# Moving one PSUM copy behind four exponentials in ScalarE's order, in both attention loops

## What is computed

```python
x = x + tanh(g_xattn[0]) * _L0_xattn_ref(_layernorm(x), ctx, ctx, mask, ...)
x = x + tanh(g_ffn[0]) * _L0_ffn_ref(_layernorm(x), ...)       # 64 experts, top 6
x = x + tanh(g_xattn[1]) * _L1_xattn_ref(_layernorm(x), ctx, ctx, bias, ...)
x = x + tanh(g_ffn[1]) * _L1_ffn_ref(_layernorm(x), ...)       # 8 experts, each takes its best tokens
# in both attentions:
scores = einsum('bhqd,bhkd->bhqk', qh, kh) / sqrt(8)           # masked, or with a bias
attn = softmax(scores, axis=-1)
out = einsum('bhqk,bhkd->bhqd', attn, vh)
```

## Time and profile before

| | |
|---|---|
| three timed runs | 939.1 us median (938.69 to 942.69) |
| the profiled execution | 940.7 us |
| its span, first to last instruction | 938.9 us |
| busy, whole span | PE 77%, DVE 72%, POOL 65%, ACT 52% |
| stretch 81 to 231 us (rolled part of loop 0, 150.00 us): busy | PE 138.50, DVE 136.74, ACT 123.28, POOL 104.03 us |
| stretch 481 to 647 us (rolled part of loop 1, 166.00 us): busy | PE 152.36, DVE 139.83, POOL 136.61, ACT 132.58 us |
| granted TensorE clock | 0.99 in the first of these stretches, 1.00 in the second |

### The profile page before, as it was taken

How to read it: one execution, slowest core, us unless ns; L and a number is a source line. 1 busy time by engine, 2 the same in 40 slices (tenths; PEclk the granted TensorE clock), 3 DMA queues, 4 the chain that set the end, 5 groups by cost and what they waited for, 6 DMA issues and landing times. The chain is left out here.

```text
span 938.9 us, 23770 instructions
## 1 busy us (share of the span) xinstructions
PE 719.0 (77%) x6259; PEld 494.9 (53%) x6259; DVE 673.6 (72%) x2225; ACT 492.1 (52%) x1719; POOL 611.7 (65%) x1109
## 2 busy tenths in 40 slices
PE   3888999999847998358999999999810379879770
PEld 2555556566533666335666666666510157557560
DVE  3787999999966664147888888888769756775334
ACT  2886888878831112037777787777700032432320
POOL 4888666666633676367888888888310376777772
PEclk9999999999967999579999999999955589999895
DMA  6111222222222333133334444333100225665568
GB/s 178 61 66 52 83 83 87 75 75 75 93 66 71 104 106 102 34 114 126 119 118 140 139 142 141 126 125 123 71 12 0 72 52 161 185 167 165 164 182 235
DMA packets 98731, 100.61 MB, mean 107 GB/s; under 512 B 24511, under 2 KB 76077, under 8 KB 98659
## 3 DMA queue, kind: packets, MB, share of 16 engines
q1 hardware_dynamic: 88306, 88.25, 30.2%
q0 software_dynamic: 6656, 9.66, 3.7%
q10 hardware_dynamic: 3696, 1.84, 0.7%
HBM read 60.84 MB, written 44.17 MB: 112 GB/s over the span
## 5 line engine op out<-in xcount | busy, mean ns | idle before, releaser
L563 ACT ACTIVATE P<-bank,mx 128x120 f32<-128x120 f32 x1024 | 277.5, 433 | 4.0 <-DVE mx L865 3.9
L466 PE MATMUL bank<-ident,P 128*120 128x128 f32 x1024 | 167.4, 286 | 41.6 <-ACT P L563 39.3
L466 PEld LDWEIGHTS bank<-ident,P 128*120 128x120 f32 x1024 | 106.1, 138 | 131.2 <-issue 75.2
L865 DVE TENSOR_REDUCE mx<-bank 128x4 f32<-128x480 f32 x256 | 150.5, 650 | 20.8 <-PE bank L455 17.3
L1748 POOL DMA_INDIRECT xg<-token_rows,tokens x64 | 66.7, 1042 | 70.1 <-DVE tokens L1802 51.2
L446 PE MATMUL bank<-bp,identr 128*128 128x480 f32 x256 | 87.3, 426 | 0.0
L1758 POOL DMA_INDIRECT expert_sums<-y,sum_rows x64 | 70.6, 1103 | 23.5 <-issue 18.6
L665 POOL TENSOR_TENSOR Km<-Kf,kmask 128x480 f32<-128x480 f32 x64 | 63.3, 989 | 29.8 <-ACT Kf L547 29.1
L480 PE MATMUL bank<-PT,Vb 120*32 120x128 f32 x2048 | 82.3, 279 | 0.0
L630 POOL TENSOR_TENSOR rstd<-rs,minus_half 128x1 f32<-128x1 f32 x128 | 72.6, 567 | 10.7
L575 ACT ACTIVATE PT<-bank,kept 120x512 f32<-120x512 f32 x64 | 45.2, 706 | 57.8 <-issue 43.0
(11 more groups left out here) (244 smaller groups left out, 1707.7 us busy)
## 6 DMA issues: line engine op xcount, KB each, us to landing
expert_sums<-zeros SPq DMA_DIRECT2D x32, 512.0 KB, 3.4
choice_rows<-zeros SPq DMA_DIRECT2D x32, 384.0 KB, 2.4
yrows<-choice_rows SPq DMA_DIRECT2D x32, 384.0 KB, 3.1
XT<-expert_sums SPq DMA_DIRECT2D x16, 512.0 KB, 5.8
XS<-expert_sums SPq DMA_DIRECT2D x16, 512.0 KB, 5.5
w<-in_w13T SPq DMA_DIRECT2D x8, 704.0 KB, 4.2
token_rows<-payload SPq DMA_DIRECT2D x32, 128.0 KB, 1.7
ctx<-in_ctxT SPq DMA_DIRECT2D x64, 60.0 KB, 2.0
```

The lines of the kernel that those rows point to most:

```text
L466: mm = nc.tensor.transpose(TB[r % 2][0:KV, S * j:S * j + S], t.P[:, r, j, :], t.ident[:])
L563: e = nc.scalar.activation(t.P[:, r, j, :], heads(SC[r])[:, j, :], ACT.Exp, bias=t.mx[:, G * r + j:G * r + j + 1], scale=-1.0)
L865: ve.tensor_reduce(t.mx[:, G * r:G * r + G], heads(SC[r]), AX.X, ALU.min).then_inc(ev.mins, 1)
```

## The change

In ScalarE's `step`, the copy of the last turned group of batch i-1, `keep_turned(on(i, -1), 3)`, comes behind the four exponentials of group 0 of batch i instead of in front of them. Exponentials of group 1 follow it as before. No wait, signal, buffer or instruction is added or taken away, and no other engine's order changes.

```diff
             def step(i, k):
                 u, w = k % 2, (k + 1) % 2
                 here = on(i, 0)
+                if here is not None:
+                    exponentials(here, 0)
                 if on(i, -1) is not None:
                     keep_turned(on(i, -1), 3)
                 if here is not None:
-                    exponentials(here, 0)
                     exponentials(here, 1)
                 if on(i, 1) is not None:
                     keep_projections(on(i, 1), w, (k + 1) % 4)
```

## The result

| | before | changed |
|---|---|---|
| timed runs, median us | 938.89 (935.5 to 942.69, 4 runs) | 954.78 (949.39 to 956.26, 4 runs) |
| ratio, 95% interval | | 1.0143 (1.0093 to 1.0193) |
| profiled execution, us | 940.7 | 956.26 |
| span, us | 938.9 | 954.5 |

The changed kernel is slower by 15.9 us of the median, and the interval of the ratio lies wholly above 1. The forecast was 956, 946 to 963.

The account below looks back on a forecast made before the run. The prediction took a ring through ScalarE's exponentials, turn 2, project_out and VectorE's residual to bound both attention loops. Its terms, 2.6 + 2.0 + 1.0 + 10.8 + 0.9 = 17.3 us on the 939.1 median, gave 956, range 946 to 963.

Parts of the forecast that it names:

- the sum: Delays over all steps of both attention loops: 2.6 + 2.0 + 1.0 + 10.8 + 0.9 = 17.3 us.
- Two steps of loop 1: Sign: reduce to reduce, two steps grow from 16.8 to about 17.9 us; under 17.2 the forecast is wrong.
- The ring: Both loops: reduce, exponentials 0 to 2, turn 2, project_out, residual, next reduce; 7.49 us a turn in loop 0.
- the hidden place: ScalarE's idle time before the first minima, hiding 0.06 us of the copy in loop 0 and 0.39 in loop 1.
- Term (b): The copy between exponentials 0 and 1 has no idle time to hide it; costs 0.50 us in loop 0, 0.58 in loop 1.
- Term (a): Exponentials 0 start a release after the first minima: 0.03 us in unrolled steps, 0.11 in rolled ones.
- The gain at the front: Turn 0 and VectorE's copy of it come earlier, only 0.07 us in loop 0; counted at nothing.
- Reader of the copy: TensorE's values(before, 3) reads the copy; in loop 0 it ends at 153.2, before TensorE gets there at 153.7.
- faster: Rival: VectorE and TensorE set the pace, VectorE's gap before its turn 0 copy closes; 19 us gained, 920; chance 0.04.
- no change: Rival: the copy's new place is absorbed between exponentials 1 and the residual, front gain cancels the rest; 939; chance 0.07.
- Only loop 1 pays: Rival: VectorE's own order in loop 0 may take up the 0.17; sum 11.7 us, so 951; chance 0.14.
- More: Rival: release 0.19 in rolled steps, and breaking the eight exponentials costs up to 0.09 a step; 965; chance 0.10.

Follow-up runs that it names:

- early turn: Turn 3 moved from the head of TensorE's next step to before scores(after): on the kernel before 0.9979 of before, on the changed kernel 1.0294.
- short copies: From batch 1 on only 128 of 512 columns of group 3 copied: changed kernel 0.9961 of before, kernel before 0.9895.
- values by VectorE: Kernel before with the projected values copied by VectorE instead of ScalarE: both loops 0.988 of before, loop 1 only 0.9958.
- short copy in front: Kernel before, copy left in front of exponentials 0 but only 128 of 512 columns from batch 1 on: 0.9895 of before, loop 1 step 8.06 us.
- the two loops alone: Copy moved in one loop only, against the kernel before: loop 0 only 1.0048 of before, loop 1 only 1.0129.

## Why the prediction was right

The direction and the size came out: 956 forecast, 954.78 measured. The mechanism, the copy's place on ScalarE behind the minima, is shown. That the size is as near as 1.2 us is partly luck: the loops grew by 13.6 us and not by the 17.3 of the sum, and 2.1 us came from a stretch that the change does not touch. Two steps of loop 1 took 592.52 - 574.92 = 17.60, above the 17.2 that would have refuted the forecast and under its 17.9. By its own steps:

**The ring and the hidden place: shown.** ScalarE's stretch from the minima to the later exponentials is on the path of every step of both loops (short copies, values by VectorE), and the time before the minima is not (short copy in front, loop 1). Moving the copy traded one for the other.

**Term (b), the copy's place: right within 0.03.** Taken as 0.50 and 0.58, it measured 154.55 - 154.08 = 0.47 in loop 0 and 577.16 - 576.60 = 0.56 in loop 1. As an estimate from the Trainium skill, "ScalarE: Activation LUTs", section "What ACT_TABLE_LOAD costs", it would have been 0.52 and 0.61; the runs are below both. The copy itself takes 0.61 in loop 0, so its neighbour starts 0.14 before its end, where the estimate has 0.09.

**Term (a), the release in rolled steps: mis-sized.** It was taken as 0.11 and is 0.03 in the plain steps. That gives 0.03 + 0.50 - 0.44 = 0.09 for a plain step of loop 0, measured 0.07, and 0.03 + 0.58 - 0.19 = 0.42 in loop 1, measured 0.41. The 0.11 of the earlier trace rows belongs to the first step of each four, where it was 0.13 in the changed kernel. This is two thirds of the gap between the sum of 17.3 and the 3.6 + 10.0 = 13.6 us that the loops really grew by: the rolled steps that are not the first of their four, 15 in each loop, times 0.08 make 2.4. Most of the rest lies in the unrolled steps of loop 0, which cost 0.4 us together and not 1.0. That the median moved by 15.9 owes something to the spread outside the loops; the interval of the ratio, 8.7 to 18.1 us of 939, holds both.

**Which leg closes the ring: wrong for loop 0.** The prediction let it close through turn 2, project_out and the residual in both loops, and read VectorE's statistics as running into the next reduce without a gap; there is one of 0.10. The early turn showed that in loop 0 it closes through exponentials 3 and the scores; the other leg is about 0.1 behind. Exponentials 2 and 3 are moved alike, so the sum did not feel it; a change that touches only one of the legs would have. It is also why the residual of loop 0 does not wait longer, as the prediction wanted.

**The gain at the front: nothing, as said.** Turn 0 came 154.52 - 152.40 = 2.12 after the reduce, before 153.04 - 150.78 = 2.26; that is 0.14 sooner, twice the 0.07 of the prediction, and none of it reached the end of the step.

**Reader of the copy: it waits in some steps, at no cost.** The two steps shown of the changed kernel have no wait of TensorE's values for it. In the first step of each rolled four of loop 0 there is one, which the prediction did not see; the waits of the changed kernel from 100 to 250 us have
```profile
PEld bank L480 <- ACT PT L571: 1.2, 4, 0.3
```
In these steps TensorE waits for exponentials 1 and 2 afterwards, and they grew by 0.49, from 7.17 to 7.66, where the prediction had 0.50. The longer wait of 0.50 in the kernel with the copy behind exponentials 1 was free too.

Of the rivals, "faster" and "no change" fell with the two loops alone. "Only loop 1 pays", with 11.7 us, was nearer to the growth of the loops than the forecast, for the wrong cause: loop 0 pays 3.6 us, two thirds of its term of 5.6. "More" fell: the release was shorter, not longer, and breaking the row of eight exponentials added no gap (153.09 to 154.08 is four places of 0.25).

## What to carry to other kernels

An engine that is not the busiest can still hold the pace by one stretch of its order (ScalarE was busy 52% of the span and 80 to 82% of the rolled loops, TensorE 92%): find the moment at which it starts to be waited for, and keep out of the stretch behind that moment whatever can stand in the idle time before it. A copy placed in front of such a stretch costs only what sticks out; behind its first instruction it costs all. The same reading tells where to take work off: 0.16 us of ScalarE's time given to the busier VectorE, which waits elsewhere, made a plain step shorter by 0.17. And a ring can have two legs that are nearly equal: look for the second before trusting a change that shortens one.

## What the runs showed of the hardware

The four groups of scores are eight matmul records of 32 rows. The profile merges them to one block of 1.09 us; in two windows of the kernel before they stand apart, four that start together and four more 0.50 us later:
```profile
149.68 0.69 PE L455 MATMUL bank<-Km,qf 32*128 32x480 f32 x4
...
150.18 0.58 PE L455 MATMUL bank<-Km,qf 32*128 32x480 f32 x4
```
The program has one matmul for each group, so presumably each group has one record in either four, and the groups run side by side. The first reduce waits for the first group alone. In the traces of all thirteen kernels it never started less than 1.07 us after the block's start, also where VectorE stood idle for it (0.53, early turn). So the first group's result came about when the last one's did.

From the end of the first reduce to the start of the exponentials that wait for it, it took 0.03 us where nothing else was in the way, in loops whose waited values come from registers too. In the first step of a rolled four it took 0.13 (changed kernel, loop 0: reduce from 144.74 to 145.40, exponentials at 145.53); why, no run shows.
